# A decoder's second attention in another order: batch by batch over all heads, two heads a step

## The chip, the cores and the metric

One of the cores of a Trainium2 chip runs the whole program in one launch. The metric is the device time of a run in microseconds. The engines are named as the profile names them: PE (TensorE, with PEld for its weight loads), DVE (VectorE), ACT (ScalarE), POOL (GpSimd) and SP (SyncE).

## The reference

Two decoder layers, each of a self attention, a second mixing block and a feed forward part, each followed by a residual and a layer norm. The change lies at the start of the second layer: the norm that closes the first layer's mixture of experts, and the second layer's attention with 16 query heads in 4 groups of keys and values, on 4 batches of 256 tokens:

```python
x = _layernorm(x + _L0_ffn_ref(x, ...), axis=-1)          # top 4 of 32 experts a token
x = _layernorm(x + _L1_attn_ref(x, w_q, w_kv, w_dense), axis=-1)

def _L1_attn_ref(x, w_q, w_kv, w_dense):                  # x: (4, 256, 256)
    HEADS, GROUPS, KVC = (16, 4, 128)
    q = jnp.einsum('bsh,he->bse', x, w_q).reshape(b, sq, GROUPS, HPG, KVC)
    k, v = jnp.split(jnp.einsum('bsh,he->bse', x, w_kv), 2, axis=-1)
    scores = jnp.einsum('bqgpd,bkgd->bgqpk', q, k) * (SCALE / LAYER_INDEX)
    scores = jnp.where(causal[None, None, :, None, :], scores, -jnp.inf)
    probs = jax.nn.softmax(scores, axis=-1).astype(x.dtype)
    ctx = jnp.einsum('bgqpk,bkgd->bqgpd', probs, v).reshape(b, sq, HEADS * KVC)
    return jnp.einsum('bse,eh->bsh', ctx, w_dense)
```

## The kernel before

The program is a chain of functions, one for each stage, and each ends with a barrier of the engines. `layer1_attention` (L1211) does two things at once. It finishes the layer before: for each of the 8 tiles of 128 tokens, POOL fetches the token's four expert rows from memory by index (`gather`, four indirect DMAs a tile), DVE adds them with their weights (`add`), ACT squares (`ln.squares`), POOL turns the variance into a factor (`ln.power`), and DVE applies it (`ln.apply`). And it runs the attention up to the mixed values; the projection behind it is the next function.

The attention is a loop over 64 units. A unit is one head of one batch: PE makes the scores (L344, L345), DVE masks them and takes the maxima (L352), ACT the exponentials (L358, L360), DVE divides, PE turns the probabilities two units later (L269) and ACT copies them (L310), PE mixes the values three units later (L278, L279), DVE keeps the result. Each engine has its instructions in the order in which the Python code writes them, and waits on semaphores; nothing is reordered by a scheduler.

Beside the units PE has jobs, written by hand into the list `beside`: x (turn a tile of normed tokens), v (its values, 512 columns), k or kb (keys of a group for a half, 512 columns, or for one batch, 256 columns) and q or qb (queries of a head for a half or for a batch). A job goes into one of two PSUM buffers, and ACT copies it out (`keep`). Query products are made of two parts: ACT rounds the weights (`cut_high`, w_high), POOL subtracts (`cut_low`, w_low; DVE for the first two), and a product is three matmuls for each half of the contraction (L80, L81, L82). A step's weight slice, 128 KB, is loaded by SP into one of two buffers.

The order of units before: the first four units are heads 0 and 1 of batch 0, then of batch 1, with narrow products; from then on a step is one head for two batches, first all heads for batches 0 and 1, then all heads for batches 2 and 3. So tiles 0 to 3 are fetched, added and normed ahead of the loop or in its first units, and tiles 4 to 7 beside units 2 to 20. On PE the query product of step s stands in unit 2(s-1), and it waits for w_low, step s:

```python
pe.wait_ge(w_low, which + 1)
```

On POOL a fetch, a power and a low part stand in one queue, in the order of the code at L1298 to L1325. Between the weight loads of SP, behind step 6, stand the loads of the next stages (`layer1_loads`), and behind step 20 one more.

Of the kernel before, what the change touches and what calls it, by code (L numbers as in the profile page):

```python
# [8 lines left out]
P = 128  # L9
# [1201 lines left out]
def layer1_attention(nc, k, I):  # L1211
# [4 lines left out]
    STEPS = 2 * H  # L1216
    with ExitStack() as stack:
        m = Memory(nc, stack)
        kT, v = k.kT1, k.v1
        w = m.sb("a1_w", [P, 2, DC, HD])  # L1220
        w_p, x_p = Parts(m, "a1_w", [P, 2, DC, HD]), k.c_p
        q = k.y[:, 0:4, :]
# [12 lines left out]
        EARLY = 4  # L1235
        first = [("x", 0), ("v", 0), ("x", 1), ("v", 1), ("kb", (0, 0)), ("qb", (0, 0)), ("qb", (1, 0)),
                 ("x", 2)]
        later = [("x", 4), ("v", 4), ("x", 5), ("v", 5), ("x", 6), ("v", 6), ("x", 7), ("v", 7),
                 ("k", 4), ("k", 5), ("k", 6), ("k", 7)]
        beside = [[] for _ in range(UNITS)]  # L1240
        beside[0] = [("v", 2), ("kb", (1, 0))]
        beside[1] = [("x", 3), ("kb", (2, 0)), ("kb", (3, 0)), ("kb", (0, 1)), ("qb", (0, 1)), ("qb", (1, 1)), ("v", 3)]
        beside[3] = [("kb", (1, 1))]
        beside[5] = [("kb", (2, 1)), ("kb", (3, 1))]
        for u in range(2, UNITS):
            if u % 2 == 0 and u // 2 + 1 < STEPS:
                beside[u].append(("q", u // 2 + 1))
            elif u >= 7 and (u - 7) // 2 < len(later):
                beside[u].append(later[(u - 7) // 2])
        number = {job: i for i, job in enumerate(first + [job for jobs in beside for job in jobs])}  # L1250
        ADD, SQUARE, APPLY, LOW = ({first_u + 4 * t: 4 + t for t in range(4)} for first_u in (2, 3, 5, 8))
# [5 lines left out]
        def of(u):  # L1257

            if u < EARLY:
                return u % 2, u % 2, u // 2  # L1260
            return u // 2, u // 2 % H, u // (2 * H) * 2 + u % 2

        def q_job(u):

            step, head, b = of(u)
            return number["qb", (head, b)] if u < EARLY else number["q", step]

        with nc.Block() as block:
            @block.sync
            def _(sp):  # L1270
                for step in range(STEPS):
                    at_least(sp, w_low, step - 1)
                    head = step % H
                    sp.dma_start(w[:, step % 2], I["L1_attn_w_q"][:, head * HD:(head + 1) * HD
# [4 lines left out]
                    if step == 20:  # L1279
                        sp.wait_ge(job_kept, number["k", 7] + 1)  # L1280
                        sp.dma_start(k.spread_w, I["spread"]).then_inc(k.spread_in, 16)
# [5 lines left out]
            def _(pool):  # L1287
                def gather(t):
                    for j in range(TOP0):
                        pool.indirect_dma_start(got(t, j), None, k.out_slots[:, :],  # L1290
                                                bass.IndirectOffsetOnAxis(k.from_slot[:, t, j:j + 1], 0)
                                                ).then_inc(fetched[t], 16)

                def cut_low(step):
                    pool.wait_ge(w_high, step + 1)
                    pool.tensor_tensor(w_p.l[:, step % 2], w[:, step % 2], w_p.h[:, step % 2], ALU.subtract  # L1296
# [3 lines left out]
                ln.power(pool, 0)  # L1300
                gather(2)
                ln.power(pool, 1)
                gather(3)
                ln.power(pool, 2)
                ln.power(pool, 3)
                gather(4)
                cut_low(2)
                gather(5)
                cut_low(3)
                ln.power(pool, 4)  # L1310
                gather(6)
                cut_low(4)
                cut_low(5)
                gather(7)
                ln.power(pool, 5)
                cut_low(6)
                cut_low(7)
                ln.power(pool, 6)
                cut_low(8)
                cut_low(9)  # L1320
                ln.power(pool, 7)
                for step in range(10, STEPS):
# [3 lines left out]
            def _(pe):  # L1326
                def job(kind, which):
# [15 lines left out]
                    elif kind == "kb":  # L1343
                        g, b = which
                        pe.wait_ge(k.xT_ready, xT_base + 2 * b + 2)
# [3 lines left out]
                    elif kind == "qb":  # L1349
                        step, b = which  # L1350
                        pe.wait_ge(w_low, step + 1)
                        pe.wait_ge(x_low, 2 * b + 2)
                        for c in range(DC):
                            last = product(pe, out[:, 0:S], w_p[:, step, c, :], x_p[:, c, b * S:(b + 1) * S],
                                           c == 0, c == DC - 1)
                    elif kind == "k":
                        half, g = divmod(which, GROUPS)
                        pe.wait_ge(k.xT_ready, xT_base + 4 * half + 4)
                        for c in range(DC):
                            last = pe.matmul(out, k.w_kv[:, c, g * HD:(g + 1) * HD],  # L1360
                                             k.xT[:, c, half * HALF:(half + 1) * HALF], start=c == 0, stop=c == DC - 1)
                    else:
                        half = which // H
                        pe.wait_ge(w_low, which + 1)
                        pe.wait_ge(x_low, 4 * half + 4)
                        for c in range(DC):
                            last = product(pe, out, w_p[:, which % 2, c, :], x_p[:, c, half * HALF:(half + 1) * HALF],
# [1893 lines left out]
```

## Time and profile before

| what | value |
|---|---|
| median of 3 runs | 1102.95 us (1102.59 to 1107.55) |
| the profiled execution | 1101.99 us |
| its span, first to last instruction | 1100.0 us |
| PE busy | 999.1 us, 91% |
| DVE, ACT, POOL busy | 711.0, 606.7, 462.0 us |
| mean granted clock of PE | 0.961 |

The span is the time between the first and the last instruction of the profiled execution; what is left of its time lies around it. The granted clock is a share of 2.4 GHz, and it has two levels, 1 and 0.5 (1.2 GHz). Busy shares of the whole span are averages over stages with different limits, so the stage that the change touches is read by itself below. In the rows in order of time, the number in brackets at the end is the engine's idle time ahead of the instruction, with what ended it.

### The profile page before, as it was taken

The page shows a single profiled execution, that of the slowest core. Times are in us where ns is not written, and L with a number is a line of the kernel's source. Part 1 is how long each engine was busy: PE and PEld are TensorE (multiplying, and loading weights), DVE is VectorE, ACT ScalarE, POOL GpSimd, SP SyncE. Part 2 cuts the span into 40 slices and gives each one's busy share as a digit, 9 for nine tenths or more (in the row PEclk, how much of TensorE's full clock was granted, in tenths as well). Part 3 has the DMA queues.
Part 4 walks back from the last instruction along what each step waited for, and adds up shares of the span by engine and source line. Part 5 has one row for each costly group of instructions (what it writes and reads, how often), then busy time and mean ns, then how long its engine had stood idle before and what let it go on. Part 6 is the DMA issues. An engine that isn't in the chain of part 4 may idle for free. (4 is left out here: it accounts for less than half of the span.)

```text
span 1100.0 us, 18924 instructions
## 1 busy us (share of the span) xinstructions
PE 999.1 (91%) x6064; PEld 816.5 (74%) x6064; DVE 711.0 (65%) x2102; ACT 606.7 (55%) x1650; POOL 462.0 (42%) x473
## 2 busy tenths in 40 slices
PE   7999999998995699849899999988878889999996
PEld 6898889887883589727778888965444568777775
DVE  5766676663576356535665667646797557888886
ACT  3656655655222255426666776547785546555553
POOL 5787767761367444366211110210137214444321
PEclk9999999999997799959999999998998999999999
DMA  6732111000011699733400111001003011112101
GB/s 201 256 127 80 30 30 30 15 15 2 1 44 56 193 341 335 255 96 85 155 25 26 63 30 40 1 23 51 2 1 117 1 58 58 58 58 66 51 1 39
DMA packets 83784, 85.61 MB, mean 78 GB/s; under 512 B 8577, under 2 KB 75975, under 8 KB 83568
## 3 DMA queue, kind: packets, MB, share of 16 engines
q1 hardware_dynamic: 79776, 75.59, 21.0%
q0 software_dynamic: 3072, 7.34, 2.2%
q10 hardware_dynamic: 848, 1.57, 0.4%
q8 instruction: 47, 0.77, 0.3%
q14 instruction: 41, 0.34, 0.1%
HBM read 63.36 MB, written 22.02 MB: 78 GB/s over the span
## 5 line engine op out<-in xcount | busy, mean ns | idle before, releaser
L579 POOL TENSOR_TENSOR a_qk<-h,a_by_sin 128x512 f32<-128x512 f32 x64 | 81.8, 1278 | 5.0
L352 DVE CUSTOM_DVE_ANT_0 h<-a_score_ps,mask_bf 128x128 f32<-128x128 f32 (+1 forms) x128 | 40.7, 355 | 62.1 <-PE a_score_ps L345 62.1
L1296 POOL TENSOR_TENSOR a_w_l<-a_w,a_w_h 128x256 fp32r<-128x256 f32 x30 | 21.8, 728 | 113.4 <-ACT a_w_h L1489 113.2
L358 ACT ACTIVATE y_moe<-y_moe,a_nmax 128x128 f32<-128x128 f32 x64 | 25.6, 400 | 75.5 <-DVE a_nmax L352 75.5
L459 PEld LDWEIGHTS a_proj_ps<-a_w,xT 128*128 128x128 f32 x512 | 62.5, 193 | 2.7 <-issue 0.6
L1035 POOL TENSOR_TENSOR e_w_l<-e_w,e_w_h 128x512 fp32r<-128x512 f32 x32 | 40.8, 1275 | 52.6 <-ACT e_w_h L1103 52.6
L459 PE MATMUL a_proj_ps<-a_w,xT 128*128 128x128 f32 x512 | 62.6, 276 | 0.2 <-DVE hT L517 0.2
L80 PE MATMUL a_proj_ps<-a_x_l,a_w_h 128*128 128x512 f32 x128 | 58.4, 456 | 3.4 <-POOL a_w_l L584 3.4
L759 PE MATMUL t_y_ps<-wo,attnT 128*128 128x256 f32 x256 | 57.6, 381 | 0.0
L2639 POOL TENSOR_TENSOR m_up_l<-m_up_w,m_up_h 128x1024 fp32r<-128x1024 f32 x8 | 19.5, 2436 | 89.4 <-ACT m_up_h L2611 89.4
L358 ACT ACTIVATE h<-h,a_nmax 128x128 f32<-128x128 f32 x64 | 25.7, 401 | 48.4 <-DVE a_nmax L352 48.4
L352 DVE CUSTOM_DVE_ANT_0 y_moe<-a_score_ps,mask_bf 128x128 f32<-128x128 f32 (+1 forms) x128 | 40.6, 353 | 18.0 <-PE a_score_ps L345 17.5
L759 PEld LDWEIGHTS t_y_ps<-wo,attnT 128*128 128x128 f32 x256 | 47.8, 190 | 5.9
L82 PE MATMUL a_proj_ps<-a_x_h,a_w_l 128*128 128x512 f32 x128 | 51.5, 403 | 0.0
L81 PE MATMUL a_proj_ps<-a_x_h,a_w_h 128*128 128x512 f32 x128 | 50.9, 398 | 0.0
L513 DVE TENSOR_TENSOR h<-a_proj_ps,cos_q 128x512 f32<-128x512 f32 x32 | 22.1, 691 | 43.8 <-PE a_proj_ps L82 43.8
L517 DVE STREAM_SHUFFLE hT<-a_proj_ps 128x512 f32<-128x512 f32 x64 | 47.3, 739 | 0.0
L575 POOL TENSOR_TENSOR a_by_sin<-hT,sin_q 128x512 f32<-128x512 f32 x32 | 41.1, 1283 | 9.8 <-DVE hT L517 9.2
L2123 DVE TENSOR_TENSOR wo<-l_dec,l_qk_ps 128x384 f32<-128x384 f32 x64 | 35.1, 549 | 14.4 <-ACT l_dec L2086 13.6
L339 DVE COPY a_probsT<-a_turn_ps 128x384 f32<-128x384 f32 x64 | 34.8, 544 | 14.0 <-PE a_turn_ps L269 14.0
L575 POOL TENSOR_TENSOR a_by_sin<-hT,sin_k 128x512 f32<-128x512 f32 x32 | 41.3, 1291 | 4.5 <-DVE hT L517 4.5
L278 PE MATMUL a_mix_ps<-a_probsT,v 128*128 128x256 f32 x128 | 39.4, 390 | 3.8 <-ACT a_probsT L310 3.8
(465 smaller groups left out, 3505.5 us busy)
## 6 DMA issues: line engine op xcount, KB each, us to landing
slots<-zeros SPq DMA_DIRECT2D x4, 2048.0 KB, 8.1
e_rows<-slots SPq DMA_DIRECT2D x32, 256.0 KB, 4.3
e_w<-in_L_ffn_w_dram SPq DMA_DIRECT2D x32, 256.0 KB, 4.5
out_slots<-e_out SPq DMA_DIRECT2D x32, 256.0 KB, 4.0
e_w<-in_L_ffn_w_dram SPq DMA_DIRECT2D x32, 128.0 KB, 4.1
a_w<-in_L_attn_w_q_dram SPq DMA_DIRECT2D x32, 128.0 KB, 2.2
m_up_w<-in_up_dram SPq DMA_DIRECT2D x8, 512.0 KB, 3.6
a_w<-in_L_attn_Wq_dram SPq DMA_DIRECT2D x16, 128.0 KB, 2.2
```

Of the source, the lines that this page charges most:

```text
L80: pe.matmul(out, left[0], right[1], start=start, stop=False)
L81: pe.matmul(out, left[0], right[0], start=False, stop=False)
L82: return pe.matmul(out, left[1], right[0], start=False, stop=stop)
L278: pe.matmul(self.mix_ps[:, r, 0:S], v(0), self.probsT[:, r, 0:S], start=True, stop=False, skip_group_check=True)
L352: done = dve.tensor_tensor_reduce(self.probs[:, b, cells], self.score_ps[:, r, cells], self.k.mask_bf[:, cells], -1.0, 3e38, ALU.add, ALU. ...
L358: act.activation(self.probs[:, b, 0:P], self.probs[:, b, 0:P], ACT.Exp, bias=self.nmax[:, b, 0:1], scale=-1.0, accum_out=self.total[:, b, ...
L459: last = pe.matmul(proj_ps[:, c % 2, t * HD:(t + 1) * HD], k.xT[:, kc, half * HALF + t * P:half * HALF + (t + 1) * P], w[:, par, 2, kc, :] ...
L517: dve.stream_shuffle(swapped[:, r, :], proj_ps[:, c % 2, :], [i ^ 1 for i in range(32)]).then_inc(rot_in, 1)
L575: pool.tensor_tensor(by_sin[:, r2, :].rearrange("p (b s) -> p b s", b=2), swapped[:, r, :].rearrange("p (b s) -> p b s", b=2), sin[:, None ...
L579: pool.tensor_tensor(qk[:, par, 0 if what == "q" else 1, half * HALF:(half + 1) * HALF], by_cos[:, r, :], by_sin[:, r2, :], ALU.add).then_ ...
L759: last = pe.matmul(y_ps[:, t % 2, 0:D], k.ctxT[:, h, t * P:(t + 1) * P], k.wo[:, h, :], start=h == 0, stop=h == H - 1)
L1035: pool.tensor_tensor(w13_p.l[:, r], w13[:, r], w13_p.h[:, r], ALU.subtract).then_inc(w_low, 1)
```

## The change

The loop goes through the batches one after another, for each over all heads. A step is now a pair of heads for one batch: units 2s and 2s+1 use step s, and a step's query product is made of two products of 256 columns, one for each head, in one PSUM buffer. A weight slice is 256 KB wide, and the 8 slices are loaded four times instead of 16 slices twice. Keys and values are kept for two batches only (`KEPT`), and the memory that comes free holds the weight buffers and the queries. Only the two tiles of batch 0 are normed ahead of the loop; the tiles of batch b are fetched, added, squared and normed beside the units of batch b-1, at the same places in each. Each fetched row has a semaphore of its own, so that `add` waits for one row at a time.

```diff
+    PAIRS = H // 2
+    STEPS = B * PAIRS
+    BATCH = H
...
+        first = [("x", 0), ("v", 0), ("x", 1), ("v", 1), ("k", (0, 0)), ("q", 0), ("k", (1, 0))]
         beside = [[] for _ in range(UNITS)]
...
+        for u in range(0, UNITS, 2):
+            if u // 2 + 1 < STEPS:
                 beside[u].append(("q", u // 2 + 1))
...
+        beside[1].append(("k", (2, 0)))
+        beside[3].append(("k", (3, 0)))
+        ADD, SQUARE, APPLY, LOW = {}, {}, {}, {}
+        for b in range(1, B):
+            u = BATCH * (b - 1)
+            for i in range(QT):
+                t = QT * b + i
+                ADD[u + 2 + 4 * i], SQUARE[u + 3 + 4 * i], APPLY[u + 5 + 4 * i], LOW[u + 8 + 4 * i] = t, t, t, t
+                beside[u + 7 + 4 * i].append(("x", t))
+                beside[u + 9 + 4 * i].append(("v", t))
+            beside[u + 15] += [("k", (0, b)), ("k", (1, b))]
+            beside[u + 17].append(("k", (2, b)))
+            beside[u + 19].append(("k", (3, b)))
-        ADD, SQUARE, APPLY, LOW = ({first_u + 4 * t: 4 + t for t in range(4)} for first_u in (2, 3, 5, 8))
...
         def of(u):
+            step = u // 2
+            return step, 2 * (step % PAIRS) + u % 2, step // PAIRS
...
                     for j in range(TOP0):
                         pool.indirect_dma_start(got(t, j), None, k.out_slots[:, :],
                                                 bass.IndirectOffsetOnAxis(k.from_slot[:, t, j:j + 1], 0)
-                                                ).then_inc(fetched[t], 16)
+                                                ).then_inc(fetched[t][j], 16)
...
                 gather(0)
                 gather(1)
                 ln.power(pool, 0)
+                ln.power(pool, 1)
                 gather(2)
...
+                for b in range(1, B):
+                    step, t = PAIRS * (b - 1), QT * b
+                    if b == 1:
+                        cut_low(2)
+                    else:
+                        cut_low(step + 1)
+                        cut_low(step + 2)
+                    ln.power(pool, t)
+                    gather(t + 1)
+                    cut_low(step + 3)
+                    cut_low(step + 4)
+                    ln.power(pool, t + 1)
+                    cut_low(step + 5)
+                    if b + 1 < B:
+                        gather(t + 2)
+                    cut_low(step + 6)
+                    cut_low(step + 7)
+                    cut_low(step + 8)
+                for step in range(STEPS - PAIRS + 1, STEPS):
                     cut_low(step)
...
+                        for a in range(2):
+                            for c in range(DC):
+                                last = product(pe, out[:, a * S:(a + 1) * S], weights(which, c, a),
+                                               x_p[:, c, b * S:(b + 1) * S], c == 0, c == DC - 1)
...
                 def add(t):
-                    dve.wait_ge(fetched[t], TOP0 * 16)
                     for j in range(TOP0 - 1):
+                        dve.wait_ge(fetched[t][j], 16)
                         dve.scalar_tensor_tensor(k.y[:, t, :], got(t, j), k.weight[:, t, j:j + 1], k.y[:, t, :],
                                                  ALU.mult, ALU.add).then_inc(part, 1)
...
-                add(2)
-                ln.apply(dve, 2)
-                add(3)
                 for u in range(UNITS):
...
+                    if step == 28:
+                        sp.wait_ge(job_kept, number["k", (3, B - 1)] + 1)
```

POOL, from the fetches of tile 4 on (before): `DMA attnT<-out_slots` are a tile's four row fetches, L1296 a low part, L137 and L140 a power.

```order
L1290 DMA attnT<-out_slots,from_slot 128x256 x4
L1296 TENSOR_TENSOR a_w_l<-a_w,a_w_h 128x256
L1290 DMA attnT<-out_slots,from_slot 128x256 x4
L1296 TENSOR_TENSOR a_w_l<-a_w,a_w_h 128x256
L137 TENSOR_SCALAR ln_c_var<-ln_c_ssq 128x1
L140 TENSOR_TENSOR ln_c_rstd<-ln_c_var,minus_half 128x1
L1290 DMA attnT<-out_slots,from_slot 128x256 x4
L1296 TENSOR_TENSOR a_w_l<-a_w,a_w_h 128x256 x2
L1290 DMA attnT<-out_slots,from_slot 128x256 x4
```

POOL, from the fetches of tile 2 on (now), with L1302 for the fetches and L1308 for the low parts of steps 2, 3 and 4, 5, 6 to 10:

```order
L1302 DMA attnT<-out_slots,from_slot 128x256 x4
L1308 TENSOR_TENSOR a_w_l<-a_w,a_w_h 128x512
L137 TENSOR_SCALAR ln_c_var<-ln_c_ssq 128x1
L140 TENSOR_TENSOR ln_c_rstd<-ln_c_var,minus_half 128x1
L1302 DMA attnT<-out_slots,from_slot 128x256 x4
L1308 TENSOR_TENSOR a_w_l<-a_w,a_w_h 128x512 x2
L137 TENSOR_SCALAR ln_c_var<-ln_c_ssq 128x1
L140 TENSOR_TENSOR ln_c_rstd<-ln_c_var,minus_half 128x1
L1308 TENSOR_TENSOR a_w_l<-a_w,a_w_h 128x512
L1302 DMA attnT<-out_slots,from_slot 128x256 x4
L1308 TENSOR_TENSOR a_w_l<-a_w,a_w_h 128x512 x5
```

What moved: the power of tile 2, whose squares ACT makes in unit 3, and the fetches of tile 3 now stand ahead of the low part of step 3; the power of tile 3, squared in unit 7, stands ahead of that of step 5. Before, the power of tile 4, squared in unit 3, had the low part of step 3 ahead of it and that of step 4 behind.

PE, the end of unit 3 and the start of unit 4 with the product of step 3 (before); L1347 are keys:

```order
L1347 MATMUL a_job_ps<-xT,hT 128x256 x2
L269 MATMUL a_turn_ps<-ident,h 128x128 x3
L278 MATMUL a_mix_ps<-a_probsT,v 128x256
L279 MATMUL a_mix_ps<-a_probsT,v 128x128
L344 MATMUL a_score_ps<-kT,y_moe 128x128
L345 MATMUL a_score_ps<-kT,y_moe 128x256
L80 MATMUL a_job_ps<-c_p_l,a_w_h 128x512
L81 MATMUL a_job_ps<-c_p_h,a_w_h 128x512
L82 MATMUL a_job_ps<-c_p_h,a_w_l 128x512
```

PE, the same place (now); L1358 are the keys of group 3:

```order
L1358 MATMUL a_job_ps<-xT,hT 128x256 x2
L269 MATMUL a_turn_ps<-ident,h 128x128 x3
L278 MATMUL a_mix_ps<-a_probsT,a_v 128x256
L279 MATMUL a_mix_ps<-a_probsT,a_v 128x128
L344 MATMUL a_score_ps<-a_kT,a_q 128x128
L345 MATMUL a_score_ps<-a_kT,a_q 128x256
L80 MATMUL a_job_ps<-c_p_l,a_w_h 128x256
L81 MATMUL a_job_ps<-c_p_h,a_w_h 128x256
L82 MATMUL a_job_ps<-c_p_h,a_w_l 128x256
```

What moved: the product of step 3 stands in unit 4 in both, and it takes the weights of POOL's low part of step 3; it is now twice as many matmuls of half the width.

## Rows read from the trace of the kernel before

**Rows 1.** By stage: us, busy PE, PEld, DVE, ACT, POOL, granted clock, DMA, GB/s

```profile
467.30:494.10 26.80, 12.29 (x30) 6.52 (x31) 10.11 (x27) 7.27 (x18) 17.92 (x22) 0.55 0.33 98
494.10:599.60 105.50, 99.44 (x516) 78.52 (x515) 62.62 (x286) 68.13 (x226) 31.25 (x42) 0.98 0.24 73
599.60:671.90 72.30, 72.11 (x433) 63.08 (x432) 50.35 (x251) 54.22 (x187) 10.19 (x14) 1.00 0.13 40
```

**Rows 2.** PE in order of time (start, us, engine, line, operation), second half

```profile
665.08 0.39 PE L344 MATMUL a_score_ps<-kT,y_moe 128*128 128x128 f32 x2
...
665.55 0.58 PE L80 MATMUL a_job_ps<-c_p_l,a_w_h 128*128 128x512 f32 x1
...
667.12 0.49 PE L269 MATMUL a_turn_ps<-ident,h 128*128 128x128 f32 x3
...
668.10 0.39 PE L344 MATMUL a_score_ps<-kT,y_moe 128*128 128x128 f32 x2
...
669.74 0.39 PE L344 MATMUL a_score_ps<-kT,y_moe 128*128 128x128 f32 x2
```

**Rows 3.** PE in order of time, first half: narrow products, keys, one turned tile

```profile
499.84 2.91 PE L1347 MATMUL a_job_ps<-xT,hT 128*128 128x256 f32 x12
...
502.40 0.47 PE L80 MATMUL a_job_ps<-c_p_l,a_w_h 128*128 128x256 f32 x1
...
504.04 1.89 PE L1341 MATMUL a_job_ps<-hT,xT 128*128 128x512 f32 x4
...
549.20 0.39 PE L344 MATMUL a_score_ps<-kT,y_moe 128*128 128x128 f32 x2
...
551.06 0.39 PE L344 MATMUL a_score_ps<-kT,y_moe 128*128 128x128 f32 x2
```

**Rows 4.** POOL and PE in order of time: power, four fetches, low part, product

```profile
512.88 0.21 POOL L137 TENSOR_SCALAR ln_c_var<-ln_c_ssq 128x1 f32<-128x1 f32 x1 [1.41 <-ACT ln_c_sq L131]
...
513.92 1.01 POOL L1290 DMA_INDIRECT attnT<-out_slots,from_slot  x1 [0.18 <-issue]
...
517.74 0.94 POOL L1290 DMA_INDIRECT attnT<-out_slots,from_slot  x1 [0.30 <-issue]
...
518.71 0.74 POOL L1296 TENSOR_TENSOR a_w_l<-a_w,a_w_h 128x256 fp32r<-128x256 f32 x1
...
519.54 0.47 PE L80 MATMUL a_job_ps<-c_p_l,a_w_h 128*128 128x512 f32 x1 [1.34 <-issue]
```

**Rows 5.** Unit 10 and the power behind its add: PE, DVE, ACT, POOL

```profile
530.22 0.39 PE L344 MATMUL a_score_ps<-kT,y_moe 128*128 128x128 f32 x2
...
535.50 0.08 DVE L352 DVE_READ_ACCUMULATOR2_ANT a_nmax<- 128x1 f32 x1
...
537.40 0.40 ACT L358 ACTIVATE h<-h,a_nmax 128x128 f32<-128x128 f32 x1
...
539.88 0.19 POOL L137 TENSOR_SCALAR ln_c_var<-ln_c_ssq 128x1 f32<-128x1 f32 x1 [2.43 <-ACT ln_c_sq L131]
```

**Rows 6.** Low and high parts of 128x512 elsewhere: page's groups, ACT in time

```profile
L1035 POOL TENSOR_TENSOR e_w_l<-e_w,e_w_h 128x512 fp32r<-128x512 f32 x32 | 40.8, 1275 | 52.6 <-ACT e_w_h L1103 52.6
...
456.12 0.63 ACT L1103 ACTIVATE e_w_h<-e_w 128x512 fp32r<-128x512 f32 x1
```

**Rows 7.** A wait of PE, ACT's before it, and the clock behind (by stage)

```profile
536.24 0.42 ACT L1489 ACTIVATE a_w_h<-a_w 128x256 fp32r<-128x256 f32 x1 [3.38 <-DMA a_w<-in_L_attn_w_q_dram]
...
537.57 1.22 PE L278 MATMUL a_mix_ps<-a_probsT,v 128*128 128x256 f32 x2 [2.96 <-ACT a_probsT L310]
...
537.00:538.00 1.00, 0.43 (x1) 0.43 (x2) 0.00 (x0) 1.00 (x5) 0.45 (x1) 0.60 0.00 0
...
540.00:541.00 1.00, 1.00 (x5) 0.82 (x4) 0.35 (x3) 0.00 (x0) 0.62 (x2) 0.70 0.00 0
```

**Rows 8.** Ahead of the loop, in order of time: POOL's power, PE's turn

```profile
484.24 0.19 POOL L137 TENSOR_SCALAR ln_c_var<-ln_c_ssq 128x1 f32<-128x1 f32 x1
...
485.72 0.66 PE L1334 MATMUL a_job_ps<-ident,x 128*128 128x128 f32 x2 [1.23 <-DVE x L146]
```

More of the change, by code:

```diff
@@ L1257, in of, with keys, value @@
         def of(u):
[L1259 to L1266, printed above, removed]
+            step = u // 2
+            return step, 2 * (step % PAIRS) + u % 2, step // PAIRS
+        def keys(b, i, j):
+            return slice(b % KEPT * S + i, b % KEPT * S + j)
+        def value(t):
+            return t % (KEPT * QT)
         with nc.Block() as block:
@@ L1348, in job, with weights @@
                                              k.xT[:, c, b * S:(b + 1) * S], start=c == 0, stop=c == DC - 1)
[L1349 to L1361, printed above, removed]
                     else:
-                        half = which // H
+                        b = which // PAIRS
                         pe.wait_ge(w_low, which + 1)
-                        pe.wait_ge(x_low, 4 * half + 4)
-                        for c in range(DC):
-                            last = product(pe, out, w_p[:, which % 2, c, :], x_p[:, c, half * HALF:(half + 1) * HALF],
-                                           c == 0, c == DC - 1)
+                        pe.wait_ge(x_low, QT * b + QT)
+                        for a in range(2):
+                            for c in range(DC):
+                                last = product(pe, out[:, a * S:(a + 1) * S], weights(which, c, a),
+                                               x_p[:, c, b * S:(b + 1) * S], c == 0, c == DC - 1)
                     last.then_inc(job_done, 1)
+                def weights(step, c, a):
+                    return (w_h[:, step % 2, c, a * HD:(a + 1) * HD], w_l[:, step % 2, c, a * HD:(a + 1) * HD])
                 def mix(u):
@@ L1373, in mix @@
                     g = head // HPG
-                    at.mix(pe, u, u % 4, lambda j: v[:, 2 * b + j, g * HD:(g + 1) * HD])
+                    at.mix(pe, u, u % 4, lambda j: v[:, value(QT * b + j), g * HD:(g + 1) * HD])
                 for one in first:
@@ L1466, in keep @@
                     elif kind == "v":
-                        done = act.activation(v[:, which, :], from_, ACT.Copy)
-                    elif kind == "kb":
+                        done = act.activation(v[:, value(which), :], from_, ACT.Copy)
+                    elif kind == "k":
                         g, b = which
-                        done = act.activation(kT[:, g, b * S:(b + 1) * S], from_[:, 0:S], ACT.Copy)
-                    elif kind == "qb":
-                        step, b = which
-                        done = act.activation(q[:, 2 * b + step, :], from_[:, 0:S], ACT.Copy, scale=HD ** -0.5)
-                    elif kind == "k":
-                        half, g = divmod(which, GROUPS)
-                        done = act.activation(kT[:, g, half * HALF:(half + 1) * HALF], from_, ACT.Copy)
+                        done = act.activation(kT[:, g, keys(b, 0, S)], from_[:, 0:S], ACT.Copy)
                     else:
@@ L1497, in _ @@
                 keep("v", 0)
-                keep("x", 1)
-                keep("v", 1)
-                ln.squares(act, 2)
-                for one in first[-4:]:
+                for one in first[2:]:
                     keep(*one)
-                ln.squares(act, 3)
+                cut_high(2)
                 for u in range(UNITS):
```

84 lines of the change are left out of this document (22 added, 62 removed).

## The prediction

> **What bounds the kernel now.** I read the times by stage first, then the order in time of the stage that the diff touches, then the waits in it. The edited function's loop of 64 units (one head of one batch each) runs from about 494.1 to 671.9 us of the span, with a first half of 105.50 and a second of 72.30 us [rows 1]. In the second half of the loop TensorE is busy 72.11 of 72.30 us, while VectorE, ScalarE and GpSimd have idle time, GpSimd most (10.19 us busy) [rows 1]. There the loop costs what TensorE's instructions cost: a unit with a query product lasts 3.02 us (665.08 to 668.10), one without 1.64 us (668.10 to 669.74), and the product starts 0.47 us after its unit's scores [rows 2]. In the first half TensorE has 99.44 busy us of 105.50: 6.1 us of idle time, the largest piece 2.96 us ahead of a mix at 537.57, after which the clock stood at its 1.2 GHz level until about 540.7 [rows 1, 7]. That mix waited for ScalarE, and ScalarE had waited 3.38 us for a weight slice [rows 7]. A second wait is small but tells more: a query product started at 519.54, just behind the end of GpSimd's low part at 518.71 + 0.74, which had stood behind four row fetches [rows 4]. GpSimd's queue can hold TensorE.
>
> **What the change does to the work.** A step's query product becomes 12 matmuls of 256 columns instead of 6 of 512. The 6 take 1.57 us (665.55 to 667.12) [rows 2]; 12 of 256 columns took 1.64 us with one seam between two products in them (502.40 to 504.04) [rows 3], without it about 1.62. That is +0.05 us in some 30 steps, **+1.5 us**. The Trainium skill (TensorE: Matmul & The Clock Gate, Back-to-back issue gap) gives N / 2.4 + 2.5 ns for an isolated gap; by it the 6 more gaps cost 15 ns a step, and the sum would be 1 us lower. The rows differ from it, and they decide.
>
> Keys now come in 256 columns everywhere: three such products took 2.91 us, 0.97 each [rows 3]; the four of 512 columns that go cost about two of these each, so nothing changes. One token tile more (x of tile 2) is turned inside the loop: a unit with such a turn lasted 1.86 us (549.20 to 551.06) against 1.64, **+0.2 us** [rows 2, 3].
>
> ScalarE's high part and GpSimd's low part of the weights are now 128x512: 0.63 us instead of 0.42, and 1.275 us instead of 0.74 [rows 4, 6, 7]. ScalarE has 18 us to spare in 72 [rows 1], the 0.2 us a step fits. Twice the weight bytes are read; at 40 GB/s in the second half [rows 1], with a step's slice asked for two steps ahead, I cost that at nothing. The wait for the slice at 536.24 came from the other loads queued ahead of it; in the new kernel these go out while TensorE stands (below), so that wait goes.
>
> **Before the loop.** The adds can start on the first row, and the second tile's power no longer stands behind a fetch (it ran at 484.24), so x of tile 1 can start when TensorE has finished the tile before instead of after 1.23 us of idle time at 485.72 [rows 8]. But a fourth product, k of group 1, is put ahead of the first scores (0.97 us, more at 1.2 GHz), and the first scores now wait for one 512 wide copy. I take **0** for the first scores' time, with ends of -2 (clock up earlier) and +1.
>
> **The waits that the change makes.** GpSimd's new queue is, for each following batch: ..., power of its first tile, four fetches, low part s+3, low part s+4, power of its second tile, low part s+5, ... with s = 8(b-1). The order listing shows it. The squares that a power waits for are issued by ScalarE at the end of unit 16(b-1)+3; the product s+3 that needs the next low part is TensorE's in unit 16(b-1)+4, one unit later. Before, the same kind of power stood two or three units ahead of the low part's use. What is queued behind: on GpSimd everything, on TensorE the turn, mix and scores of all later units, and so VectorE and ScalarE.
>
> The length, from a unit that had an add, unit 10, scores at S = 530.22 [rows 5]. The add of a tile stands between its maxima and those of unit 11, which ended at 535.50 + 0.08, so S + 5.36. With ScalarE free, its exponentials follow at once; from their start to the power it took 537.40 to 539.88, 2.48 us (exponentials, a copied job, the copied probabilities, the squares). So a power starts at **S + 7.9**.
>
> First kind (the power with four fetches behind it): from power to low part 512.88 to 518.71, 5.83 us, of which four fetches at 1.27 [rows 4]; the low part 1.28 [rows 6]; 0.09 to TensorE [rows 4]. The product starts at S + 15.1. TensorE could start it at S + 3.07 + (1.64 + 0.97) + 0.47 = S + 6.15. **Stall 8.9 us**, once for each of batches 1, 2, 3.
>
> Second kind (power, then low part s+5): 7.9 + 1.04 (512.88 to 513.92) + 1.28 + 0.09 = S + 10.3, against S + 3.07 + 1.86 + 0.47 = S + 5.4. **Stall 4.9 us**, three times. The four fetches behind it and the low part after them end at about S + 10.2 + 5.1 + 1.3 = S + 16.6; TensorE, with a unit of 3.02 and one with a 512 wide value product (about 3.3) to do first, comes there no sooner, so I count no third stall.
>
> Together 3 x 8.9 + 3 x 4.9 = **+41.4 us**. An error of 1 us in S + 7.9 moves this by 6 us.
>
> The clock: after the 2.96 us idle at 537.57 TensorE ran about 3.1 us at half speed, a loss of 1.5 us [rows 7]. Each of the six stalls is longer. I take 1.5 us for each, **+9.0 us**; ends 0 (clock not lowered) and 3 us each.
>
> What goes: the idle 6.1 us of the first half and its 1.5 us of half clock, and 0.2 us in the second half: **-7.8 us** [rows 1, 7].
>
> **The sum.** 1.5 + 0.2 - 7.8 + 41.4 + 9.0 = +44.3 us on the profiled execution's 1101.99 us (span 1100.0, 2.0 around it; 0.96 under the median): **1146 us**.
>
> **The rivals.** (a) The cut is on time. The mechanism is the place of the power in GpSimd's queue; if the low parts came before TensorE asks, the six stalls and their clock (50.4 us) would be gone while the 7.8 us of old waits still go: 1102 - 7.8 + 1.7 = 1096, faster than before. It decides at a power at S - 1.0 (first kind) and S + 5.4 - 2.4 = S + 3.0 (second); the rows put it at S + 7.9. For it: GpSimd is mostly idle. Against: the add itself ends after S + 4. (b) Fetches cost GpSimd little. Then power to low part takes 1.04 instead of 5.83 us, the first kind is 4.1 us, 14.4 us less: 1132. The Trainium skill (DMA: Bandwidth & Descriptors, Anatomy of one DMA, SWDGE path) calls descriptor generation "small, variable" and most of a DMA's fixed cost completion; by that rule (b) holds. Against it the rows: the fetches start 1.27 us apart, and the low part starts only after the last. (c) The clock stays low longer after the long stalls. In the 26.8 us before the loop the mean granted clock was 0.55, so it was half for some 24 us although TensorE worked in 12.3 of them [rows 1]; if each long stall were followed by as much work at 1.2 GHz, about 6.2 us instead of 1.5 would be lost three times, +14: 1160. Against: behind a stall TensorE has a full queue.
>
> **How the numbers follow.** Forecast 0.72, (c) 0.13, (b) 0.08, (a) 0.05, and 0.02 for a time within 0.5% of before, by several stalls missing. A measurement of this kernel can tell about 0.5%, 5.5 us, from no change. Range: down, the clock not lowered (-9), the chain 1 us shorter (-6), the start (-2): 1129, which also takes in (b); up, the clock at 3 us each (+9), the chain 1 us longer (+6), the start (+1): 1162, which takes in (c). Faster 0.05, same 0.02, slower 0.93.
>
> **What would show it.** Six stretches without TensorE inside the loop, at the products of steps 3, 5, 11, 13, 19, 21, each ending 0.1 us behind a low part on GpSimd, long and short in turn, near 9 and 5 us; GpSimd waiting for ScalarE's squares ahead of each power; a lowered clock behind each; the wait at the slice of step 7 gone; units 52 to 60 in pairs of 4.71 us. It would be wrong if GpSimd's low part of step 11 were done before unit 20's scores, or if a fetch let the next instruction start early.

## The result, and the profile of the changed kernel

The changed kernel takes 1147.18 us (median; 1143.73 to 1148.57), the kernel before beside it 1102.77 us: a ratio of 1.0387, 95% interval 1.0358 to 1.0417, so 3.9% slower. The forecast was 1146, with a range of 1129 to 1162. The profiled execution of the changed kernel took 1143.73 us (span 1141.6), 41.7 us more than that of the kernel before (1101.99).

By stage (columns as in [rows 1]) the changed kernel reads:

```profile
467.10:489.40 22.30, 9.67 (x33) 5.35 (x33) 7.04 (x18) 6.37 (x16) 13.14 (x16) 0.64 0.39 119
489.40:609.60 120.20, 93.79 (x564) 83.38 (x564) 58.12 (x273) 65.10 (x210) 37.91 (x39) 0.89 0.26 80
609.60:712.40 102.80, 89.49 (x578) 81.03 (x577) 55.89 (x271) 63.64 (x208) 24.59 (x23) 0.93 0.16 49
```

The loop of 64 units, from the first scores to the last, takes 223.0 us (489.40 to 712.43), before 177.8. TensorE was busy all but 6.3 of those 177.8 us [rows 1]; now it is idle for 39.7 us of 223.0, and its clock, 0.98 and 1.00 before, is 0.89 and 0.93. The stage ahead of the loop, from the first row fetch to the first scores, is 3.6 us shorter (22.3 against 25.9). The page's group of the query products names nearly all of that idle time, and TensorE in order of time shows it as six waits, long and short in turn (the third and fourth, left out, are 8.49 us at 569.32 and 4.62 at 586.72):

```profile
L80 PE MATMUL a_job_ps<-c_p_l,a_w_h 128*128 128x256 f32 x128 | 44.7, 349 | 39.4 <-issue 39.4
```

```profile
507.37 0.55 PE L80 MATMUL a_job_ps<-c_p_l,a_w_h 128*128 128x256 f32 x1 [8.54 <-issue]
...
523.64 0.36 PE L80 MATMUL a_job_ps<-c_p_l,a_w_h 128*128 128x256 f32 x1 [4.63 <-issue]
...
633.43 0.55 PE L80 MATMUL a_job_ps<-c_p_l,a_w_h 128*128 128x256 f32 x1 [8.49 <-issue]
...
649.53 0.55 PE L80 MATMUL a_job_ps<-c_p_l,a_w_h 128*128 128x256 f32 x1 [4.63 <-issue]
```

"issue" means that the profile names no releaser. GpSimd in order of time does; this is its queue ahead of the first two waits, and it is the counterpart of [rows 4]:

```profile
500.19 0.19 POOL L137 TENSOR_SCALAR ln_c_var<-ln_c_ssq 128x1 f32<-128x1 f32 x1 [8.31 <-ACT ln_c_sq L131]
500.47 0.56 POOL L140 TENSOR_TENSOR ln_c_rstd<-ln_c_var,minus_half 128x1 f32<-128x1 f32 x1
501.22 1.02 POOL L1302 DMA_INDIRECT attnT<-out_slots,from_slot  x1 [0.19 <-issue]
...
505.04 0.94 POOL L1302 DMA_INDIRECT attnT<-out_slots,from_slot  x1 [0.30 <-issue]
505.99 1.28 POOL L1308 TENSOR_TENSOR a_w_l<-a_w,a_w_h 128x512 fp32r<-128x512 f32 x1
...
521.25 0.40 POOL L137 TENSOR_SCALAR ln_c_var<-ln_c_ssq 128x1 f32<-128x1 f32 x1 [12.76 <-ACT ln_c_sq L131]
...
522.28 1.25 POOL L1308 TENSOR_TENSOR a_w_l<-a_w,a_w_h 128x512 fp32r<-128x512 f32 x1
```

GpSimd stands idle for 8.31 us, waiting for ScalarE's squares; then power, four fetches and low part follow, the low part ends at 507.27, and the product starts at 507.37. In the second wait the fetches are not in between: power, low part, product at 523.64.

TensorE's granted clock (next to last but two, as in [rows 7]) behind the first wait:

```profile
507.00:508.00 1.00, 0.63 (x3) 0.66 (x4) 0.00 (x0) 0.00 (x0) 1.00 (x2) 0.50 0.20 74
...
510.00:511.00 1.00, 1.00 (x7) 0.95 (x6) 0.00 (x0) 0.69 (x2) 0.00 (x0) 0.79 0.99 228
511.00:512.00 1.00, 1.00 (x9) 0.90 (x8) 0.00 (x0) 0.28 (x1) 0.00 (x0) 1.00 0.77 260
```

After the restart at 507.37 TensorE runs at 0.50, its 1.2 GHz level, until about 510.4. Behind the six restarts the clock stands at 0.50 for 3.1 to 6.0 us each, 25.6 us together.

### The profile page after: what moved, and what is told of

Its sections match the earlier page's. It is cut to its first block and busy times, and to the rows that moved or that the text cites. A ratio compares the mean times of both kernels' runs of the same rounds, so it can differ in the third digit from the quotient of the medians.

```text
span 1141.6 us, 19345 instructions
## 1 busy us (share of the span) xinstructions
PE 1008.4 (88%) x6260; PEld 837.5 (73%) x6260; DVE 708.8 (62%) x2102; ACT 613.1 (54%) x1652; POOL 478.2 (42%) x473
## 5 line engine op out<-in xcount | busy, mean ns | idle before, releaser
L278 PE MATMUL a_mix_ps<-a_probsT,a_v 128*128 128x256 f32 x256 | 79.6, 394 | 0.5 <-ACT a_probsT L310 0.4
L80 PE MATMUL a_job_ps<-c_p_l,a_w_h 128*128 128x256 f32 x128 | 44.7, 349 | 39.4 <-issue 39.4
L1308 POOL TENSOR_TENSOR a_w_l<-a_w,a_w_h 128x512 fp32r<-128x512 f32 x30 | 37.9, 1271 | 84.8 <-ACT a_w_h L1476 84.7
L358 ACT ACTIVATE y_moe<-y_moe,a_nmax 128x128 f32<-128x128 f32 x64 | 25.6, 400 | 75.7 <-DVE a_nmax L352 75.7
L80 PEld LDWEIGHTS a_job_ps<-c_p_l,a_w_h 128*128 128x128 f32 x128 | 27.2, 213 | 42.5 <-issue 41.6
L279 PEld LDWEIGHTS a_mix_ps<-a_probsT,a_v 128*128 128x128 f32 x256 | 49.6, 194 | 7.1
L352 DVE CUSTOM_DVE_ANT_0 y_moe<-a_score_ps,mask_bf 128x128 f32<-128x128 f32 (+1 forms) x128 | 40.6, 353 | 18.0 <-PE a_score_ps L345 17.5
L279 PE MATMUL a_mix_ps<-a_probsT,a_v 128*128 128x128 f32 x256 | 49.7, 276 | 0.0
```

The costliest lines, as they stand in the source:

```text
L80: pe.matmul(out, left[0], right[1], start=start, stop=False)
L278: pe.matmul(self.mix_ps[:, r, 0:S], v(0), self.probsT[:, r, 0:S], start=True, stop=False, skip_group_check=True)
L279: pe.matmul(self.mix_ps[:, r, P:S], v(1), self.probsT[:, r, S:CAUSAL], start=False, stop=True, skip_group_check=True).then_inc(self.mixed, 1)
L352: done = dve.tensor_tensor_reduce(self.probs[:, b, cells], self.score_ps[:, r, cells], self.k.mask_bf[:, cells], -1.0, 3e38, ALU.add, ALU. ...
L358: act.activation(self.probs[:, b, 0:P], self.probs[:, b, 0:P], ACT.Exp, bias=self.nmax[:, b, 0:1], scale=-1.0, accum_out=self.total[:, b, ...
```

## Experiments

The loop lengths below are from the profiled execution of each kernel (first to last scores); ratios are to the kernel before, measured beside each kernel (its own median moved between 1101.05 and 1103.66 us), and one below 1 is faster. "Both" is the changed kernel with both moves in GpSimd's queue.

| kernel | median us | ratio, 95% interval | loop us |
|---|---|---|---|
| before | 1102.77 | | 177.8 |
| changed | 1147.18 | 1.0387 (1.0358 to 1.0417) | 223.0 |
| fetches earlier | 1137.12 | 1.0297 (1.0262 to 1.0332) | 208.5 |
| powers later | 1117.58 | 1.0111 (1.0074 to 1.0148) | 196.8 |
| both | 1100.66 | 0.9973 (0.9950 to 0.9995) | 176.7 |
| both, loads spread | 1101.02 | 0.9975 (0.9956 to 0.9994) | 176.8 |
| changed, stalls filled | 1137.85 | 1.0344 (1.0301 to 1.0386) | 211.7 |
| before, loads spread | 1097.47 | 0.9958 (0.9939 to 0.9977) | 173.7 |
| both, semaphore per tile | 1099.86 | 0.9980 (0.9954 to 1.0007) | 177.1 |
| both, adds split | 1098.10 | 0.9966 (0.9939 to 0.9994) | 174.1 |
| both, copies reordered | 1098.70 | 0.9970 (0.9943 to 0.9998) | 175.0 |
| both, adds split, copies reordered | 1096.35 | 0.9943 (0.9920 to 0.9966) | 173.3 |

**The fetches alone.** Theory: TensorE waits for whatever stands ahead of the low part in GpSimd's queue, each instruction at its length. Rivals: a fetch costs GpSimd little; the wider weight parts cost the time.

```diff
                     else:
                         cut_low(step + 1)
+                        gather(t + 1, (0, 1))
                         cut_low(step + 2)
+                        gather(t + 1, (2, 3))
                     ln.power(pool, t)
-                    gather(t + 1)
                     cut_low(step + 3)
```

> The changed kernel with one edit: in GpSimd's queue the four fetches of a batch's second tile move from behind the power of the first tile to the places around the low parts s+1 and s+2, two and two. The powers stay ahead of the low parts s+3 and s+5. Theory (TensorE is held by GpSimd's queue, and each instruction that stands between the squares and the low part costs its length): the three long stalls lose the four fetches, about 4.8 us each, and go from 8.5 to about 3.7 us; the three short ones stay at 4.6. Time 1147 - 14 = about 1133 us (1128 to 1137). Rival A (a fetch occupies GpSimd only little, the long stalls are long for another reason, such as the squares of a first tile coming later): long stalls stay at 8.5 us, 1145 to 1149. Rival B (the time went into the wider high and low parts and the doubled weight bytes): no change, 1145 to 1149.

TensorE in order of time, the first two waits (the other four: 3.48, 4.61, 3.48, 4.61):

```profile
502.47 0.36 PE L80 MATMUL a_job_ps<-c_p_l,a_w_h 128*128 128x256 f32 x1 [3.55 <-issue]
...
518.97 0.55 PE L80 MATMUL a_job_ps<-c_p_l,a_w_h 128*128 128x256 f32 x1 [4.61 <-issue]
```

The long waits lose 5.0 us each, the short ones nothing: a fetch costs the queue 1.25 us, and both rivals fall. The loop is 14.6 us shorter, as expected; the time only 10.1, so that the median, 1137.12, lies just outside the expected 1128 to 1137. In the profiled executions the missing 4 us lie behind the loop, in code that is the same in both kernels (433.4 us from the loop's end against 429.2). The largest difference of clock there is the stretch from 120 to 160 us behind the loop's end (first row the changed kernel, second this one); why it differs stays open:

```profile
832.40:872.40 40.00, 30.77 (x377) 17.94 (x375) 32.83 (x83) 31.99 (x97) 14.23 (x14) 1.00 0.01 3
```

```profile
818.00:858.00 40.00, 31.67 (x353) 17.27 (x341) 30.72 (x77) 29.69 (x92) 12.34 (x11) 0.88 0.01 2
```

**The powers alone.** Theory: a power one low part later has its squares ready in time; the fetches, still in one block, then hold the next low part.

```diff
+                    cut_low(step + 3)
                     ln.power(pool, t)
                     gather(t + 1)
-                    cut_low(step + 3)
                     cut_low(step + 4)
-                    ln.power(pool, t + 1)
                     cut_low(step + 5)
+                    ln.power(pool, t + 1)
```

> The changed kernel with one edit: in GpSimd's queue the low part s+3 goes ahead of the power of a batch's first tile, and the low part s+5 ahead of the power of the second; the four fetches stay directly behind the first power, so that they now stand ahead of the low part s+4. Theory (place in the queue): the six stalls at the products of steps s+3 and s+5 are gone. New, shorter ones: the low part s+4 stands behind a power and four fetches and the product that needs it is one step later than before, about 4 us three times; the low part s+6 behind a power and the next four fetches, about 3 us twice. Time about 1125 us (1116 to 1132). Rival A (the squares themselves come so late that every product behind them waits whatever the order): the stalls move to s+4 and s+6 at their old length, 1140 to 1150. Rival B (width of the high and low parts, weight bytes): no change.

```profile
511.27 0.55 PE L80 MATMUL a_job_ps<-c_p_l,a_w_h 128*128 128x256 f32 x1 [3.45 <-issue]
...
527.99 0.36 PE L80 MATMUL a_job_ps<-c_p_l,a_w_h 128*128 128x256 f32 x1 [2.52 <-issue]
```

The six waits are gone; five new ones, one step later, hold 15.0 us in all (3.45, 2.52, 3.46, 2.12, 3.43), against 18 expected (three of 4, two of 3). Rival A, that the squares come too late whatever the order, would have kept 39.

**Both.** Each power one low part later, each four fetches in two pairs with a low part between them.

> The changed kernel with both edits of the two runs before: each power one low part later, and every group of four fetches split in pairs with a low part between them. Theory: GpSimd's queue holds TensorE nowhere in the loop; all six stalls (39 us) and the lowered clock behind them (25.6 us at half speed, about 12.8 lost) are gone. What then comes back is the wait for the weight slice queued behind the loads for the rest of the layer, which these stalls had hidden: 3 to 4.5 us with its clock. Time 1147 - 39.4 - 12.8 + 4 = about 1099 us (1092 to 1106), no longer slower than the kernel before. Rival (half or more of the 44 us comes from the wider parts, the twofold weight bytes, or narrower matmuls): 1120 or more.

No product waits any more, as the group of the query products in this kernel shows:

```profile
L80 PE MATMUL a_job_ps<-c_p_l,a_w_h 128*128 128x256 f32 x128 | 42.0, 328 | 0.0
```

The loop is back at 176.7 us and the time no longer above the kernel before (ratio 0.9973): the whole loss was the order of GpSimd's queue. One part of the expectation failed: the wait for a weight slice did not come back. SyncE issues the slice of step 7 behind the other loads, and ScalarE takes it (the high part) 6.3 us later without a wait, where the kernel before issued it at 527.37 and had it at 536.24 [rows 7]:

```profile
514.55 3.27 SPq L1286 DMA_DIRECT2D a_w<-in_L_attn_w_q_dram  x2
```

```profile
520.89 0.61 ACT L1481 ACTIVATE a_w_h<-a_w 128x512 fp32r<-128x512 f32 x1
```

So the prediction's reason, that these loads go out while TensorE stands, was not needed. In the changed kernel it did not hold either: SyncE issued them between the first two waits, from 508.93 to 516.91 us, and the slice of step 7 only at 523.57, near the end of the second wait:

```profile
516.91 0.44 SPq L1208 DMA_DIRECT2D ones<-in_ones_dram  x1
523.57 0.38 SPq L1286 DMA_DIRECT2D a_w<-in_L_attn_w_q_dram  x1
```

What lets this slice land at least 2.5 us sooner without the stalls was not tested. The traces show one difference: in the kernel before a tile's four row fetches (from 521.28 on) go out among these loads, here the next fetch comes at 517.57, behind all of them. What is left are six waits of a mix, which the long waits had covered:

```profile
505.23 0.70 PE L278 MATMUL a_mix_ps<-a_probsT,a_v 128*128 128x256 f32 x2 [0.83 <-ACT a_probsT L310]
...
514.24 0.70 PE L278 MATMUL a_mix_ps<-a_probsT,a_v 128*128 128x256 f32 x2 [0.73 <-ACT a_probsT L310]
```

**The loads spread, in both forms.** The loads that stand behind step 6 go out in eight pieces, in the kernel of the last run and, by itself, in the kernel before.

```diff
-                    if step == 6:
-                        layer1_loads(sp, k, I)
+                    if 6 <= step < 14:
+                        layer1_loads(sp, k, I, step - 6)
```

> The kernel of the run before, and the loads for the rest of the layer, which SyncE issues in one go at step 6, spread over the steps 6 to 13 in eight pieces. Theory: the wait of ScalarE for the weight slice of step 7 or 8 goes, and the lowered clock behind it: 3 to 4.5 us less than the run before, about 1095 us (1090 to 1100), faster than the kernel before by 0.5% or a little more. Rival (that wait does not come back without the stalls, since nothing queued there is late): the same time as the run before, within 1 us.

> The kernel before with one edit: the loads for the rest of the layer, which SyncE issues in one go at step 6, are spread over the steps 6 to 13 in eight pieces. It measures by itself what the prediction put down as gone with the change: the wait for the weight slice of step 7 (3.38 us on ScalarE, 2.96 on TensorE) and the lowered clock behind it. Theory: that wait goes, 3.0 + 1.5 = 4.5 us less than the kernel before, ratio 0.996 (0.994 to 0.998). Rival (the wait is due to the fetches of rows or to the piece of weights itself, or another wait comes up in its place): ratio 0.999 to 1.002.

In the new form the edit does nothing (loop 176.8 against 176.7), since nothing waited there: the theory fails and its rival holds. In the kernel before it does what the theory said: ScalarE's high part of step 7 waits no more, the loop falls from 177.8 to 173.7 us, and the time to 0.9958 of before.

```profile
531.31 0.40 ACT L1495 ACTIVATE a_w_h<-a_w 128x256 fp32r<-128x256 f32 x1
```

**The clock by itself.** The six waits are filled with matmuls whose result is thrown away, so that they last as long and only the clock differs.

```diff
+                        if which % PAIRS in (3, 5) and which < 3 * PAIRS:
+                            keep_clock(pe, out[:, 0:S], x_p.h[:, 0, 0:P], x_p.h[:, 0, 0:S],
+                                       68 if which % PAIRS == 3 else 36)
                         pe.wait_ge(w_low, which + 1)
```

> The changed kernel, and ahead of the products of steps 3, 5, 11, 13, 19 and 21, before TensorE waits for the low part, matmuls of 256 columns whose result is thrown away (68 of them ahead of the products with the long stall, 36 ahead of those with the short one): they fill the stall and end before it ends. The stalls stay as long as they are, so that only what TensorE's clock does after them differs. In the changed kernel TensorE ran at half clock for 25.6 us after the six restarts. Theory (the stall lowers the clock, and the work behind it pays): with TensorE kept busy the clock stays at its higher level, and 25.6/2 = 12.8 us go, 1147 to about 1134 (1133 to 1139; the 9.0 of the prediction would give 1138). Rival A (the engine that sets the time behind a stall is not TensorE, the work behind it catches up anyway): 1144 to 1149. Rival B (the clock is lowered by something else than TensorE's idleness): lowered stretches stay, 1145 to 1149.

TensorE in order of time at the first wait (68 thrown-away matmuls, then the product):

```profile
499.38 8.49 PE L89 MATMUL a_job_ps<-c_p_h 128*128 128x256 f32 x68
508.24 0.39 PE L80 MATMUL a_job_ps<-c_p_l,a_w_h 128*128 128x256 f32 x1 [0.37 <-POOL a_w_l L1308]
```

```profile
507.00:508.00 1.00, 0.87 (x8) 0.67 (x6) 0.00 (x0) 0.00 (x0) 1.00 (x1) 1.00 0.30 90
```

The product starts 40.1 us after the first fetch of the stage, in the changed kernel 40.3: the wait is the same, and this time the profile names its releaser, GpSimd's low part. The clock stays at 1.00. The loop is 11.4 us shorter (211.7 against 223.0), near the 12.8 that half of 25.6 us makes; both rivals would have left it. In the medians 9.3 us are seen, by the two ratios 0.4%, under 5 us; the intervals of the ratios overlap, so the size rests on the trace.

**One semaphore per row, undone.** On the kernel with both moves, the add of a tile waits for all four rows again.

```diff
-                        dve.wait_ge(fetched[t][j], 16)
+                    dve.wait_ge(fetched[t], TOP0 * 16)
```

> The kernel with powers and fetches both moved (no stall left), and one part of the change undone: one semaphore for the four fetched rows of a tile instead of one for each, so that an add starts when the last row is there. In the changed kernel the last row of tile 0 landed at 474.8 and the first power ran at 477.1, directly behind the eighth fetch. Theory (the power is held by GpSimd's own fetches, so an add that starts with the first row gains little): the add's first three parts now start at 474.8 instead of 471.1, the squares end some 1.5 us later, of which 0.6 to 0.7 us reach the first turn of x: TensorE's wait there becomes 16.3 instead of 15.6 us, nothing changes in the loop, time 0.5 to 1 us more than with a semaphore for each row (1100.7), not to be told from it. Rival (early adds set the start): 2 to 3 us more, 1103 to 1104, and seen in the trace as a first turn 2 to 3 us later after the first fetch.

TensorE's first turn of x, and the power ahead of it on GpSimd:

```profile
479.60 0.69 PE L1350 MATMUL a_job_ps<-ident,x 128*128 128x128 f32 x2 [16.34 <-DVE x L146]
```

```profile
478.25 0.19 POOL L137 TENSOR_SCALAR ln_c_var<-ln_c_ssq 128x1 f32<-128x1 f32 x1 [0.62 <-ACT ln_c_sq L131]
```

The turn comes 12.0 us after the first fetch, in the kernel with both moves alone 11.3 (in the others with a semaphore per row 11.3 to 11.7): 0.3 to 0.7 us, since a power that had been ready behind the eighth fetch now waits 0.62 us for its squares. In the time it is not seen (ratio 0.9980 against 0.9973). The first scores came 24.9 us after the first fetch, against 21.9, but that is the clock: the run with the loads spread, which has the semaphores per row, shows 24.6 there too.

**What is left in the new form.** Two edits on the kernel with both moves: VectorE's add of four rows goes over two units; ScalarE copies the turned probabilities ahead of the high part and the unit's other copies. Together and each alone:

```diff
+                    if u + 1 in ADD:
+                        add(ADD[u + 1], (0, 1))
                     if u in ADD:
-                        add(ADD[u])
+                        add(ADD[u], (2, 3))
...
+                    if u >= at.TURN:
+                        at.keep_turned(act, u - at.TURN, (u - at.TURN) % 4)
                     if 2 <= u and u % 2 == 0 and u // 2 + 2 < STEPS:
                         cut_high(u // 2 + 2)
                     for one in beside[u]:
                         keep(*one)
-                    if u >= at.TURN:
-                        at.keep_turned(act, u - at.TURN, (u - at.TURN) % 4)
```

> The kernel with powers and fetches both moved (no stall left, 1100.7 us), with two more edits. VectorE's add of a tile is split over two units, two rows in each, and ScalarE copies the turned probabilities ahead of the high part and the other copies of a unit instead of behind them. What is left in that kernel's loop are six waits of a mix for these copies, 0.83 and 0.73 us in turn, 4.7 us together, and 0.11 us in each pair of units (4.82 against 4.71). Theory (ScalarE's wider high part and the undivided add hold the copied probabilities back): the loop of 176.7 us becomes 169 to 173 us, time about 1095 (1092 to 1098), faster than the kernel before. Rival (the high part is then 0.5 us later, GpSimd's low part too, and the product waits instead): loop 176 to 178, time 1099 to 1103.

> The first of the two edits of the run with split adds and reordered copies (1096.35 us) alone, on the kernel without stalls (1100.7 us, loop 176.7): VectorE's add of a tile is split over two units, ScalarE's order is as it was. Theory (the undivided add of four rows, 2 us of VectorE in one unit, makes the units behind it late; the six waits of 0.83 and 0.73 us come from it): the waits fall to 0.3 us or less, 3 to 5 us of the loop go, and the pairs of the last batch stay at 4.82. Loop 172 to 174, time 1096 to 1098. Rival (ScalarE's order makes the six waits, high part and query copy ahead of the probabilities): the waits stay at 0.7 to 0.8, loop 176 to 177, time 1099 to 1102.

> The second of the two edits alone, on the kernel without stalls (1100.7 us, loop 176.7): ScalarE copies the turned probabilities ahead of the high part and of the unit's other copies, VectorE's add is undivided. Theory of the run before this one (the add makes the six waits): the pairs of the last batch become 4.71 and some pairs before gain 0.1 too, the six waits shrink by less than half, loop 174 to 176, time 1098 to 1100. Rival (ScalarE's order makes the waits): they are gone, loop 172 to 174, time 1096 to 1098.

The groups of the mix by line (after the second bar: idle time ahead of it), with both moves alone, with the adds split, with the copies reordered, with both edits (in the first and the third the window ends ahead of the last three units, hence 122):

```profile
L278 PE MATMUL a_mix_ps<-a_probsT,a_v 128*128 128x256 f32 x122 | 37.8, 392 | 5.0 <-ACT a_probsT L310 5.0
```

```profile
L278 PE MATMUL a_mix_ps<-a_probsT,a_v 128*128 128x256 f32 x128 | 39.7, 392 | 3.3 <-ACT a_probsT L310 3.3
```

```profile
L278 PE MATMUL a_mix_ps<-a_probsT,a_v 128*128 128x256 f32 x122 | 37.0, 385 | 0.7 <-ACT a_probsT L310 0.7
```

```profile
L278 PE MATMUL a_mix_ps<-a_probsT,a_v 128*128 128x256 f32 x128 | 38.8, 385 | 0.5 <-ACT a_probsT L310 0.5
```

Together they take 1096.35 us, within the expected 1092 to 1098 and 0.6% under the kernel before; the loop of 173.3 is just above the expected 169 to 173. Alone, neither theory holds as it stood: the split leaves three of the waits at 0.79 to 1.07 us, so the add does not make them all; the new order removes the waits, but the loop gains only 1.8 us, since the units with the add stay long (4.00 us where it was 4.08) and the three units with two key products grew (3.73 us where it was 3.37). Both have a share. The pairs in the last batch go from 4.82 to 4.71 with the new order and not with the split.

## Why the prediction was right, step by step

**The bound and the place.** GpSimd's queue holds TensorE: right, and shown by undoing it. All six waits stand at the products of steps 3, 5, 11, 13, 19 and 21.

**The length of the waits.** Predicted 8.9 and 4.9 us, 41.4 together; measured 8.5 and 4.6, 39.4. The power was put at S + 7.9; it ran at S + 7.1 to 7.6 in the first kind and S + 8.1 to 8.4 in the second. From power to low part, 5.83 was predicted from [rows 4], 5.80 to 5.90 measured (500.19 to 505.99 the first time).

**The fetches.** Rival (b) falls: four of them held 5.0 us of each long wait, 1.25 a fetch. The Trainium skill (DMA: Bandwidth & Descriptors, Anatomy of one DMA, SWDGE path) calls descriptor generation "small, variable" in this path. The trace does not agree: a fetch held the queue for about as long as a whole low part (1.28 us), and nearly the same each time.

**The clock.** Predicted 9.0 us, measured 11.4. The mis-sized step is the 1.5 us for each wait: [rows 7] was a shorter wait with 3.1 us of half clock behind it, and behind two of the six (the restarts at 569.32 and 586.72) it lasted 6.0 and 5.6 us. The stretch behind the third wait reads:

```profile
574.00:575.00 1.00, 1.00 (x5) 0.91 (x5) 0.00 (x0) 0.00 (x0) 0.00 (x0) 0.50 0.00 0
575.00:576.00 1.00, 1.00 (x6) 0.76 (x6) 0.44 (x3) 0.00 (x0) 0.00 (x0) 0.86 0.00 0
```

Rival (c) named the direction; its size, 6.2 us at each long wait, was too much.

**What goes.** The 7.8 us went, and the run on the kernel before gives 4.1 us of them (loop 177.8 to 173.7) for the slice alone, 4.5 worked out. The reason given for it was wrong (above), so this term was right by luck in part.

**The steady state.** Predicted +1.5 and +0.2 us, and pairs (a unit with a product and one without) of 4.71; measured 4.82. The product is as predicted (a unit with one is 3.07 against 3.02): +0.05 a step. An estimate from the isolated gap that the Trainium skill gives (TensorE: Matmul & The Clock Gate, Back-to-back issue gap), 2.5 ns for each of six more matmuls, is 0.015 us a step; the trace does not agree. From one such unit to the next, TensorE's scores in the last batch of the changed kernel:

```profile
686.27 0.39 PE L344 MATMUL a_score_ps<-a_kT,a_q 128*128 128x128 f32 x2
...
689.34 0.39 PE L344 MATMUL a_score_ps<-a_kT,a_q 128*128 128x128 f32 x2
...
691.09 0.39 PE L344 MATMUL a_score_ps<-a_kT,a_q 128*128 128x128 f32 x2
```

The second gap is 1.75 us and not the 1.64 of [rows 2]. The 0.11 is the step that called ScalarE's wider high part fitting because ScalarE has idle time: it has, but the copy of the probabilities stands behind it in the queue. The new order of copies makes it 4.71. It is the same mistake in small as the edit itself: room on an engine is not room ahead of one instruction.

**Before the loop.** Predicted 0 with ends of -2 (clock up earlier) and +1; the first scores came 22.3 us after the first fetch, before 25.9: -3.6, outside the ends. 1.4 us are the second tile's turn (16.1 against 17.5 us after the first fetch), which no longer waits behind fetches; most of the rest is the clock, up at about 483.1 instead of 492.8.

```profile
483.00:484.00 1.00, 0.52 (x3) 0.14 (x1) 0.00 (x0) 0.66 (x2) 0.69 (x2) 0.94 0.09 20
```

```profile
492.00:493.00 1.00, 1.00 (x6) 0.91 (x6) 0.22 (x1) 0.38 (x1) 0.66 (x2) 0.59 0.00 0
```

**The sum.** In the loop 39.4 + 11.4 + 1.7 - 7.8 = 44.7 of the 45.3 us measured; the ScalarE term is in the 0.6 left. With -3.6 ahead of the loop that is 41.7, what the two profiled executions differ by. The forecast had +44.3: it had the waits 2.0 us too long and the clock behind them 2.4 too short, which nearly cancels, and the start was 3.6 off. That the two medians lie 44.4 us apart, the forecast to a tenth, is luck. Rival (a), 1096 us with the cut on time, is what the last kernel took (1096.35), but only after VectorE's add and ScalarE's order were mended too; with the cut on time alone it was 1100.66.

## What to carry to other kernels

On an engine that runs its queue in order, look at what an instruction stands behind, not at how busy the engine is: a mostly idle GpSimd held TensorE for 39 us because a wait for late squares stood ahead of a cut that was already possible. Put the instruction with the late input behind those that others wait for, and spread indirect fetches, 1.25 us of queue each, between them. A wait that leaves the critical engine idle costs its length and then the slow clock behind it, here 11.4 us on 39.4; and the new form, once mended, can't be told from the old with one group of loads mended (1096.35 and 1097.47, ratios with overlapping intervals), so the gain hoped for from a larger rewrite is to be set against the small fix.

## What the hardware showed that was not expected

The clock's rise ahead of the loop is not settled by the program alone. After the first turn at about 478 to 481 us TensorE works with nearly the same instructions in all kernels of the new form; in seven of the ten the first scores came 21.9 to 22.4 us after the first fetch (the clock was up at 483.1 in the changed kernel, at 484.4 with both moves), in three (loads spread, semaphore per tile, copies reordered) 24.6 to 24.9 us, with the clock up at 488.8 to 489.4. These are two executions side by side, both moves alone and with the loads spread, whose code up to there is the same:

```profile
487.00:488.00 1.00, 1.00 (x4) 0.48 (x3) 0.00 (x0) 0.00 (x0) 0.94 (x1) 1.00 0.45 127
```

```profile
487.00:488.00 1.00, 1.00 (x3) 0.35 (x2) 0.00 (x0) 0.00 (x0) 0.95 (x1) 0.50 0.45 135
```

These two lie 2.7 us apart with the same code, so as much of the 3.6 us gained at the start may be no property of the change; the old form, seen in two executions, took 25.9 and 25.1 us, both with the clock up late (492.8 and 489.8). The code behind the loop, the same in all kernels but for how a few loads are waited for, took 427.4 to 433.4 us in the profiled executions, with stretches at 0.88 in one and 1.00 in another; what decides it stays open. A change of one stage is better read from that stage than from the total.
